# A decoder block on one core: attention's probabilities times values as three rounded products instead of one float32 product

## What is computed

```
x = x + attn(layernorm(x)); x = x + xattn(layernorm(x), ctx, ctx); x = x + ffn(layernorm(x))

# attn:
qkv = x @ qkv_w.T + qkv_b;  q, k, v = split(qkv);  q, k = rope(q), rope(k)
logits = einsum('bqhmd,bkhd->bhmqk', q, k) * SM_SCALE            # masked above the diagonal
m = max(logits);  e = exp(logits - m);  exp_sink = exp(s - m)
w = e / (sum(e) + exp_sink)
out = einsum('bhmqk,bkhd->bqhmd', w, v)                          # the product that changes
return out @ out_w.T + out_b
```

## Time and profile before

| what | value |
|---|---|
| median of 3 runs | 1863.8 us (1858.2 to 1870.18) |
| the profiled execution | 1864.66 us, span 1862.5 us |
| granted PE clock over the span | 0.974 of full |
| busy share of the span | PE 93%, PE weight load 75%, DVE 64%, POOL 45%, ACT 44% |
| one steady body of the attention | 27.34 us |

### The profile page before, as it was taken

The page is one execution under the profiler, slowest core; times in us unless marked ns, Lnnn a source line. Parts: engine busy times, 40 slices in busy tenths (PEclk is TensorE's granted clock), DMA queues, the critical chain, the costliest instruction groups (busy, mean ns, idle before and its releaser), DMA issues. The chain is left out here.

```text
span 1862.5 us, 45291 instructions
## 1 busy us (share of the span) xinstructions
PE 1728.7 (93%) x15345; PEld 1390.9 (75%) x15441; DVE 1185.5 (64%) x2269; ACT 813.0 (44%) x1575; POOL 840.6 (45%) x1302
## 2 busy tenths in 40 slices
PE   3999999999999999999699999999995779999997
PEld 2888888888888888888577777777773779866664
DVE  5777777777777777777478888888882334422221
ACT  3334434433433444343247777777774324311111
POOL 4554655555555465555334444444444121144443
PEclk9999999999999999999879999999998799999999
DMA  5021111111112112111234444444442453222221
GB/s 183 19 58 44 42 56 54 36 51 56 42 42 56 47 37 56 56 39 42 75 101 111 123 119 117 115 118 124 123 109 63 167 207 125 74 64 67 66 64 39
DMA packets 145343, 148.43 MB, mean 80 GB/s; under 512 B 26194, under 2 KB 139926, under 8 KB 143482
## 3 DMA queue, kind: packets, MB, share of 16 engines
q1 hardware_dynamic: 138362, 120.87, 23.6%
q0 software_dynamic: 5760, 14.06, 2.4%
q10 hardware_dynamic: 1152, 12.58, 1.9%
HBM read 93.46 MB, written 54.11 MB: 79 GB/s over the span
## 5 line engine op out<-in xcount | busy, mean ns | idle before, releaser
L1149 DVE TENSOR_REDUCE xmax<-bankX 128x4 f32<-128x1024 f32 x256 | 309.2, 1218 | 63.4 <-PE bankX L1234 58.1
L1102 ACT ACTIVATE xe<-bankXT 128x512 f32<-128x512 f32 x512 | 292.1, 598 | 91.2 <-PE bankXT L1245 74.9
L1245 PE MATMUL bankXT<-stq,stk 98*128 98x256 f32 x1024 | 229.4, 310 | 11.4 <-ACT xe L1102 4.9
L369 POOL TENSOR_TENSOR roped<-ropeC,ropeD 128x512 f32<-128x512 f32 x160 | 205.4, 1290 | 56.4 <-DVE ropeD L530 56.3
L1245 PEld LDWEIGHTS bankXT<-stq,stk 98*128 98x128 f32 x1024 | 155.9, 191 | 54.1 <-ACT xe L1102 31.8
L557 DVE TENSOR_TENSOR oTl<-bankV,oTh 128x512 fp32r<-128x512 f32 x128 | 88.1, 688 | 166.7 <-ACT oTh L445 166.7
L662 PE MATMUL bankQ<-wqh,xnTh 128*128 128x512 f32 x384 | 188.9, 492 | 0.0
L1234 PE MATMUL bankX<-stk,stq 96*128 96x256 f32 x1024 | 172.6, 293 | 14.2 <-DMA rw<-in_rw 10.9
L361 POOL TENSOR_TENSOR prob<-prob,rden 128x1024 f32<-128x1024 f32 x64 | 122.0, 1906 | 88.6 <-DVE rden L553 88.6
L1234 PEld LDWEIGHTS bankX<-stk,stq 96*128 96x128 f32 x1024 | 146.2, 198 | 18.2 <-DMA rw<-in_rw 11.1
L728 PE MATMUL bankO<-woh,oTh 128*128 128x256 f32 x512 | 152.5, 298 | 0.0
(11 more groups left out here) (196 smaller groups left out, 4022.3 us busy)
## 6 DMA issues: line engine op xcount, KB each, us to landing
stackk_d<-chl SPq DMA_DIRECT2D x96, 128.0 KB, 2.3
stackq_d<-q2hl SPq DMA_DIRECT2D x96, 128.0 KB, 2.3
stk<-stackk_d SPq DMA_DIRECT2D x32, 384.0 KB
stq<-stackq_d SPq DMA_DIRECT2D x128, 96.0 KB
wexp<-in_wexp ACTq DMA_DIRECT2D x8, 1536.0 KB
x_d<-x SPq DMA_DIRECT2D x64, 128.0 KB, 1.9
xrden<-inv_d SPq DMA_DIRECT2D x64, 128.0 KB, 2.5
xin<-xg_d SPq DMA_DIRECT2D x40, 128.5 KB, 2.1
```

The costliest lines, as they stand in the source:

```text
L369: nc.gpsimd.tensor_tensor(roped[c % 3][:], ropeC[c % 2][:], ropeD[c % 2][:], ALU.add).then_inc(s_rsum, 1)
L1102: nc.scalar.activation(xe[q][:].rearrange("p n m -> p (n m)"), bT[:, q % 2, :], ACT.Exp).then_inc(s_xe, 1)
L1149: nc.vector.tensor_reduce(xmax[tile[1] % 2][:, :, a:b + 1:b - a].rearrange("p m h -> p h m"), bS[:, 2 * (pr % 2):2 * (pr % 2) + 2, :].rear ...
L1245: ins = nc.tensor.matmul(bT[:, q % 2, n * D:(n + 1) * D], stk[p][0:98, hd // 4, n * P:(n + 1) * P], stq[p][0:98, hd, :], start=True, stop= ...
```

## The change

The probabilities and the values get high and low parts. ACT writes the high part of each quarter of the transposed probabilities (probTh), DVE subtracts it from bankP to give the rest (probTl, `rest_PT`), and only that signals s_PT. v is copied to vh by ACT, DVE forms vl (`rest_v`), and ACT places both into block-diagonal tiles vbdh and vbdl (`place_v`, eight copies instead of four). `results` issues three products for each sequence in place of one float32 product. `project_out(0)` is issued in two parts with `turn_probs(2)` between them. Beside that the load of the sinks goes ahead of the weights' loads, a memset of an 8-wide tile goes from POOL to DVE in the expert stage, and two semaphores are merged there.

```
-        vbd = [[sb(f"vbd{p}{b}", [P, NKV // 2, P]) for b in range(2)] for p in range(2)]
+        vbdh = [[sb(f"vbdh{p}{b}", [P, NKV // 2, P], F32R) for b in range(2)] for p in range(2)]
+        vbdl = [[sb(f"vbdl{p}{b}", [P, NKV // 2, P], F32R) for b in range(2)] for p in range(2)]
...
 # SP, start
             sp.dma_start(bcol[:, 24:26], A["bo"].rearrange("(p c) -> p c", c=2)).then_inc(s_bias, 16)
+            sp.dma_start(sinks[:].rearrange("p r s -> p (r s)"),
+                         A["sinks"].partition_broadcast(P)).then_inc(s_bias, 16)
             for i in range(NSTAGE):
                 sp.dma_start(stage[:, i, :], wsrc[i]).then_inc(s_stage[i], 16)
-            sp.dma_start(sinks[:].rearrange("p r s -> p (r s)"),
-                         A["sinks"].partition_broadcast(P)).then_inc(s_sinks, 16)
...
 # POOL, start
             for p in range(2):
                 for b in range(2):
-                    ins = nc.gpsimd.memset(vbd[p][b][:], 0.0)
+                    nc.gpsimd.memset(vbdh[p][b][:].bitcast(F32), 0.0)
+                    ins = nc.gpsimd.memset(vbdl[p][b][:].bitcast(F32), 0.0)
             ins.then_inc(s_setg, 1)
...
 # ACT
             def evac_v(tile):
                 act.wait_ge(s_qkv, num(tile) * 6 + 6)
-                v = bk[1][:, 0, :].rearrange("p (a o d) -> p o a d", o=2, d=HD)
+                nc.scalar.activation(vh[:], bk[1][:, 0, :], ACT.Copy).then_inc(s_vh, 1)
+
+            def place_v(tile, src, dst, n):
+                if n == 0:
+                    act.wait_ge(s_vh, num(tile) + 1)
+                else:
+                    act.wait_ge(s_vl, num(tile) + 1)
+                v = src[:].bitcast(F32).rearrange("p (a o d) -> p o a d", o=2, d=HD)
                 for b in range(2):
                     for o in range(2):
-                        ins = nc.scalar.activation(vbd[tile[1]][b][o * HD:(o + 1) * HD, :, o * HD:(o + 1) * HD],
+                        ins = nc.scalar.activation(dst[tile[1]][b][o * HD:(o + 1) * HD, :, o * HD:(o + 1) * HD],
                                                    v[b * T:(b + 1) * T, o], ACT.Copy)
-                ins.then_inc(s_v, 1)
+                if n == 1:
+                    ins.then_inc(s_v, 1)
...
 # ACT, body
                 if front:
                     evac_qk(tile, 4)
+                    evac_v(tile)
                 if rear:
                     evac_O(u, 3)
                 if front:
-                    evac_v(tile)
+                    place_v(tile, vh, vbdh, 0)
+                    place_v(tile, vl, vbdl, 1)
...
 # DVE
+            def rest_PT(u, g):
+                dve.wait_ge(s_PTh, num(u) * 4 + g + 1)
+                nc.vector.tensor_tensor(probTl[g % 2][:], bP[:, 0, :].rearrange("p (a b) -> p a b", a=4),
+                                        probTh[g % 2][:].bitcast(F32), ALU.subtract).then_inc(s_PT, 1)
+
+            def rest_v(tile):
+                dve.wait_ge(s_vh, num(tile) + 1)
+                need(dve, s_v, num(tile))
+                nc.vector.tensor_tensor(vl[:], bk[1][:, 0, :], vh[:].bitcast(F32), ALU.subtract).then_inc(s_vl, 1)
...
 # PE
-                    need(pe, s_v, t)          # project, c == 1
+                    need(pe, s_vl, t)
...
-                src = probT[g % 2][:].rearrange("p j (b q) -> p j b q", b=2)
+                ph, pl = (x[g % 2][:].rearrange("p j (b q) -> p j b q", b=2) for x in (probTh, probTl))
                 for b in range(2):
-                    ins = nc.tensor.matmul(out[:, :, b, :], vbd[u[1]][b][:, g, :], src[:, :, b, :], start=True, stop=True)
+                    vhi, vlo = vbdh[u[1]][b][:, g, :], vbdl[u[1]][b][:, g, :]
+                    for n, (v, x) in enumerate(((vhi, ph), (vlo, ph), (vhi, pl))):
+                        ins = nc.tensor.matmul(out[:, :, b, :], v, x[:, :, b, :], start=(b == 0 and n == 0),
+                                               stop=(n == 2), skip_group_check=True)
...
 # PE, body
                     results(u, 1)
-                    project_out(u, 0)
+                    project_out(u, 0, (0, 1))
                     turn_probs(u, 2)
+                    project_out(u, 0, (2, 3))
```

More of the change, by code:

```diff
@@ L186, in attention @@
         prob = sb("prob", [P, 2, 16 * HD + 16])
-        probT = [sb(f"probT{g}", [P, 4, P]) for g in range(2)]
+        vh, vl = sb("vh", [P, 512], F32R), sb("vl", [P, 512], F32R)
+        probTh = [sb(f"probTh{g}", [P, 4, P], F32R) for g in range(2)]
+        probTl = [sb(f"probTl{g}", [P, 4, P], F32R) for g in range(2)]
         oTh = [sb(f"oTh{g}", [P, 4, P], F32R) for g in range(2)]
@@ L194, in attention @@
         s_bias, s_setv, s_setg = sem("s_bias"), sem("s_setv"), sem("s_setg")
-        s_bterm, s_brow, s_brows, c_bias, s_sinks = (
-            sem(n) for n in ("s_bterm", "s_brow", "s_brows", "c_bias", "s_sinks"))
+        s_bterm, s_brow, s_brows, c_bias = (
+            sem(n) for n in ("s_bterm", "s_brow", "s_brows", "c_bias"))
         s_x, s_xres, s_ctx, s_stk, s_stq, s_x1st = (
@@ L438, in evac_PT @@
                 need(act, s_pv, num(u) * 4 + g - 1)
-                nc.scalar.activation(probT[g % 2][:], bP[:, 0, :].rearrange("p (a b) -> p a b", a=4),
-                                     ACT.Copy).then_inc(s_PT, 1)
+                nc.scalar.activation(probTh[g % 2][:], bP[:, 0, :].rearrange("p (a b) -> p a b", a=4),
+                                     ACT.Copy).then_inc(s_PTh, 1)
             def evac_O(u, g):
@@ L606, in body @@
                 if rear:
+                    rest_PT(u, 0)
+                    denominator(u, 1, soft)
                     rest_O(u, 0)
-                    denominator(u, 1, soft)
+                    rest_PT(u, 1)
                 if front:
@@ L618, in body @@
                 if rear:
+                    rest_PT(u, 2)
                     rest_O(u, 2)
+                    rest_PT(u, 3)
                 if front and below(t, NT - 2):
                     norm1((h + 1, p))
+                if front:
+                    rest_v(tile)
                 if rear:
                     rest_O(u, 3)
-            dve.wait_ge(s_sinks, 16)
             stats1((0, 0))
@@ L710, in results, with project_out @@
                 out = bV[:, 0, :].rearrange("p (j b q) -> p j b q", j=4, b=2)
-                src = probT[g % 2][:].rearrange("p j (b q) -> p j b q", b=2)
+                ph, pl = (x[g % 2][:].rearrange("p j (b q) -> p j b q", b=2) for x in (probTh, probTl))
                 for b in range(2):
-                    ins = nc.tensor.matmul(out[:, :, b, :], vbd[u[1]][b][:, g, :], src[:, :, b, :], start=True, stop=True)
+                    vhi, vlo = vbdh[u[1]][b][:, g, :], vbdl[u[1]][b][:, g, :]
+                    for n, (v, x) in enumerate(((vhi, ph), (vlo, ph), (vhi, pl))):
+                        ins = nc.tensor.matmul(out[:, :, b, :], v, x[:, :, b, :], start=(b == 0 and n == 0),
+                                               stop=(n == 2), skip_group_check=True)
                 ins.then_inc(s_pv, 1)
-            def project_out(u, g):
+            def project_out(u, g, js=range(4)):
                 t = num(u)
@@ L719, in project_out @@
                 out = bO[:, 0, 0:D]
-                if g == 0:
+                if g == 0 and 0 in js:
                     if below(t, NT - 2):
@@ L725, in project_out @@
                     nc.tensor.matmul(out, onesb[:], bias3[:, 3072:3072 + D], start=True, stop=False)
-                for j in range(4):
+                for j in js:
                     for n, (a, w) in enumerate(((oTh, woh), (oTh, wol), (oTl, woh))):
@@ L729, in project_out @@
                                                stop=(g == 3 and j == 3 and n == 2))
-                ins.then_inc(s_out, 1)
+                if 3 in js:
+                    ins.then_inc(s_out, 1)
             def body(tile, front, rear, prep):
@@ L1380, in experts @@
         tok = [sb(f"tok{p}", [P, 1], I32) for p in range(2)]
-        s_w, c_tab, s_tabi, s_tabd, s_tab, s_pad, s_padd, s_ones = (
-            sem(n) for n in ("s_w", "c_tab", "s_tabi", "s_tabd", "s_tab", "s_pad", "s_padd", "s_ones8"))
+        s_w, c_tab, s_tabi, s_tab, s_pad, s_padd = (
+            sem(n) for n in ("s_w", "c_tab", "s_tabi", "s_tab", "s_pad", "s_padd"))
         s_xin, s_yst, s_x2in, s_gat, s_out = (
@@ L1457, in _ @@
         def _(pool):
-            nc.gpsimd.memset(ones8[:], 1.0).then_inc(s_ones, 1)
             def low_x(g):
@@ L1557, in _ @@
         def _(dve):
-            ch = Chain(dve, c_tab, 17, 0)
+            ch = Chain(dve, c_tab, 18, 0)
             def count_tiles():
-                dve.wait_ge(s_ones, 1)
+                ch(nc.vector.memset(ones8[:], 1.0))
                 ch(nc.vector.tensor_tensor(cnt[:], run[:], C["base"], ALU.subtract))
```

11 lines of the change are left out of this document (6 added, 5 removed).

## The result

The changed kernel takes 1894.71 us (median of 4 runs, 1891.69 to 1896.73) against 1862.96 before (4 runs): a ratio of 1.0170, interval 1.0146 to 1.0194. Forecast were 1894, a range of 1871 to 1915 and slower by over 1%. So the kernel became 1.7% slower, as forecast. The profiled execution took 1893.56 us, its span is 1891.7.

What follows compares the result with a forecast made beforehand. PE was taken to set the 27.34 us body; each of 31 bodies ends 0.95 us later (29.5), with edges of -1.5, +1.6 and +0.5 giving +30.1, about 1894 us. The range was 1871 to 1915.

Steps and rivals of the forecast that it cites:

- PE's work: In `results`, six rounded products take 0.70 us instead of 0.86 per quarter, sparing PE 0.64 a body.
- The stall before `results(0)`: At quarter 0, `rest_PT(0)` behind rope(3) on DVE stalls PE 1.44 us, plus 0.1 for an exposed weight load.
- The wait for POOL before `turn_probs(2)`: On PE at quarter 2, the existing 0.33 us wait disappears because `denominator(1)` and `norm_probs(1)` come earlier.
- cutting `project_out(0)` in two costs nothing: On PE around `turn_probs(2)`, the same twelve products and four transposes are issued, so no cost.
- The wait before `results(2)`: At quarter 2, DVE's queue from rope(4), startable 0.28 after `project(5)`, makes PE wait 0.69 us, against 0.41 before.
- `normalise(1)` at 0.41: On DVE before `results(2)`, it takes 0.41 us instead of 1.00, as POOL's `norm_probs(1)` is already over.
- Before the scores: At the body's end, `scores` waits 0.15 us for ACT's last copy, as `results(3)` is 0.16 shorter.
- The edges: Outside the steady bodies: first and last bodies -1.5 us, start's memsets and weight split +1.6, last rear +0.5.
- A: Rival: in the bodies the rest's latency is hidden and the gain is had, 1835 us; chance 0.04.
- B: Rival: only quarter 0 stalls, DVE reaching `rest_PT(2)` 0.7 us earlier; +0.2 per body, 1872 us; chance 0.10.
- C: Rival: before `results(2)`, POOL's `rope_sum(4)` takes the port before `normalise(1)`; wait grows 1.1, 1929 us; chance 0.10.
- D: Rival: PE's clock halves after waits in each body, costing over 60 us more; chance 0.03.

Runs made afterwards that it cites:

- Experiment 4: Changed kernel with two float32 products of the high parts replacing the six rounded ones in each `results`, rests still formed and waited for: 1905.35 us.
- experiment 1: Changed kernel with DVE's rest of quarter 0 formed ahead of rope(3) instead of behind it: 1876.24 us.
- experiment 2: Changed kernel without DVE's four probability subtractions, ACT's copy signalling `results` directly, low part a tile of zeros: 1823.39 us.
- Experiment 3: Changed kernel with `project_out(0)` in one piece ahead of `turn_probs(2)`: 1915.4 us.
- experiment 8: Changed kernel with float32 products for quarters 0 and 1, `turn_probs(2)` after three `project_out(0)` products, rest of quarter 2 ahead of `stats1`: 1840.96 us.
- experiment 9: Experiment 8's kernel with `project_out(2)` ahead of the first half of the scores: 1838.64 us.
- experiment 5: Changed kernel with `normalise(1)` on DVE moved ahead of rope(4), into the time of POOL's `norm_probs(1)`: 1890.79 us, one run.

## Why the prediction was right, and where it was not

The number and its main cause were right: the subtraction of quarter 0 behind rope(3) stalls PE. One step of the working was wrong, and the total is as close as it is because two terms were off in opposite directions.

**PE's work.** Forecast 0.70 for a quarter, measured 0.71 where nothing waits. Experiment 4 prices it in place: 0.42 a body.

**The stall before `results(0)`.** Forecast 1.44, and 0.1 for the exposed first load: 1.54 lost. `project(4)` ends at 655.00 + 0.23 = 655.23 and the transposes behind `results(0)` start at 657.73; less 0.70 of work that is 1.80 lost (1.65 in the other body of the loop). The mechanism was right, shown by experiments 1 and 2; the term was 0.1 to 0.26 too small. DVE took 5.05 us from the start of rope(2) to the rest (650.98 to 656.03), not 4.94, and in the longer body PE was at the next work 1.03 after the subtraction's end, not 0.86. The 0.11 on DVE is one small operation of `shift(1)`, the subtraction of 16 maxima from the sinks: 0.34 (653.43, shown above) for 0.23 before. Here it is before, and POOL's two `rope_sum` beside it, first before, then in the changed kernel:

```profile
631.45 0.23 DVE L542 TENSOR_TENSOR prob<-sinks,mx 128x16 f32<-128x16 f32 x1
...
629.11 2.54 POOL L369 TENSOR_TENSOR roped<-ropeC,ropeD 128x512 f32<-128x512 f32 x2
...
651.22 2.53 POOL L374 TENSOR_TENSOR roped<-ropeC,ropeD 128x512 f32<-128x512 f32 x2
```

In both it ends 0.02 to 0.03 behind POOL (631.68 against 631.65, 653.77 against 653.75), and where POOL is idle it takes 0.18. POOL ends 0.11 later against rope(2) in the changed kernel. The prediction took this stretch over from the rows of before with nothing added for POOL.

**The wait for POOL before `turn_probs(2)`.** Gone, as forecast. The prediction said that cutting `project_out(0)` in two costs nothing. Experiment 3 shows that it is worth 0.7 us a body; the prediction had not named this, as it put the wait that follows down to DVE's queue.

**The wait before `results(2)`: the step that failed.** "rope(4) can only start 0.28 after `project(5)`". It reads the block of `project(4)`; `project(5)` is v. rope(4) started at 659.76, right behind the rest of quarter 1 and 0.45 before `project(5)` ended. So DVE did not come late from the ropes, as the prediction had it, but waited 0.39 for ACT's copy of `results(1)`; from the end of `results(1)` on PE (660.92) to `results(2)` (663.77) the chain over ACT and DVE takes 2.85, of which PE covers 2.43 with work. The forecast of 0.69 and 0.1 compares with (663.35 to 664.58, less 0.70) 0.53 lost. So this term was 0.26 too large and the one before up to 0.26 too small; the body came out at 28.28 for 28.29 by this cancelling, which is luck, and not by the accuracy of each term. `normalise(1)` at 0.41 was right: 0.40.

**Before the scores.** Forecast 0.15. From the first product of `results(3)` to the first recorded one of the scores it is 1.24 (666.79 to 668.03) against 1.16 before (643.88 to 645.04), with 0.80 of products in place of 0.87: 0.15 more wait. The prediction's own instants for this step, 645.68 and 644.75, differ by 0.93 and not by the 0.95 that it carried on, which is 0.6 us over 31 bodies.

**The edges.** At the start the split of the weights on DVE ended 1.65 us later (forecast 1.6): the first layer-norm operation stands at 24.29 against 22.64. The last residual addition of the attention stands at 949.83 against 918.24, +31.6 (forecast 30.1). The residual additions divide it: the first one is 3.3 later (79.00 against 75.71, the 1.65 of the start included), the 27 distances that follow add 25.4, which is 0.94 each, and the last four add 2.9. The forecast had taken off 1.5 for the first and the last bodies; the last ones show a part of that, the first none. From the last addition to the end of the span it is 941.9 against 944.3; in the nine variants, which do not change that work, it was 938.0 to 946.9, so no part of the change is seen in it. These 2.4 us hide the 1.5 by which the attention was above the forecast, which is luck too.

**The rivals.** A (gain had) needed DVE earlier; experiment 2 gives its price, 1823, below the 1835 forecast, as the waits before `results(2)` go too. B didn't occur: a wait stayed before `results(2)`. It needed DVE at `rest_PT(2)` 0.7 earlier than forecast; DVE came earlier, but by less. C didn't occur: `normalise(1)` started at 660.96, POOL's `rope_sum(4)` at 661.12. D: the clock in the bodies stayed at 1.00.

What is left open: why PE takes up `results(0)` 0.06 behind the subtraction in one body of the loop and 0.25 in the other, and how much of the gain in experiments 2, 8 and 9 the order alone would bring.

## What to carry to other kernels

When a product is split into rounded terms, its price is not the terms but the extra step on the chain to them: look at what the engine that forms the rest is doing at the moment when the rest is needed, and split only those products whose rest falls into a gap of that engine. Here all of the split costs 1.7%, or 0.3% in the best order found, and the kernel with half of it, in the second half of each body, is 1.3% faster than before. Of that 1.3% under half is the products'; the rest is less waiting, most likely by the order; a change that does two things at once should be run with each of them alone, and here the order alone was not run. A sum that comes out right may be two wrong terms, so check the terms in the trace, and not only the end.

## What the runs showed of the hardware

A DVE operation of 0.40 us between SBUF tiles took 0.65 to 0.86 us in 24 of 24 records when it was issued while POOL ran a 1.91 us instruction, and ended 0.14 to 0.16 behind it in all of them (experiment 5). A DVE subtraction of 128 x 16 from SBUF takes 0.18 us beside an idle POOL, and 0.23 or 0.34 where POOL's 1.28 us addition ends within it, 0.02 to 0.04 behind POOL. Six rounded products of 256 columns with alternating stationary tiles keep the pace of 0.117 to 0.12 us each, where two float32 products of that size take 0.86. ACT's copies of 64 x 256 took 0.415 us from SBUF (four in 1.69), and 0.378 from PSUM before (four in 1.54), by the medians of 128 each.
